# Causal attention in one fused kernel: one PSUM bank for output sums, four for max tiles, maxima turned inside the score ring, value product inside the slot

## What is computed

```python
# x: (8, 1024, 256); 16 heads of 16
qkv = einsum('bte,fe->btf', query, in_proj_weight).reshape(b, t, 3, H, D)
q = q / sqrt(D)
scores = einsum('bhqd,bhkd->bhqk', q, k)
scores = where(causal, scores, -inf)
attn = softmax(scores, axis=-1)
out = einsum('bhqk,bhkd->bhqd', attn, v)
out = einsum('bte,fe->btf', out.transpose(0, 2, 1, 3).reshape(b, t, e), out_proj_weight)
```

## Time and profile before

| | us |
|---|---|
| median of 3 runs | 1429.2 |
| lowest, highest | 1426.5, 1436.69 |
| the profiled execution | 1427.34 |
| its span, first to last instruction | 1425.6 |

### The profile page before, as it was taken

One profiled execution on the slowest core, in us unless ns is written; L12 is line 12 of the kernel. 1 busy time (PEld: TensorE's weight loads), 2 busy tenths in 40 slices (PEclk: granted clock), 3 DMA queues, 4 the chain that ended last, 5 costly groups with the idle time before them and its releaser, 6 DMA issues. The chain is left out here.

```text
span 1425.6 us, 38170 instructions
## 1 busy us (share of the span) xinstructions
PE 1301.0 (91%) x9260; PEld 831.4 (58%) x9260; DVE 1177.4 (83%) x4599; ACT 908.6 (64%) x1828; POOL 458.7 (32%) x877
## 2 busy tenths in 40 slices
PE   3999999979999999999999999999999995988885
PEld 3999889845444444444444444444444443877875
DVE  4788888758899999999999999999999982778786
ACT  3666666613777777777777777777777774444442
POOL 3333433211122222222222222122123123877772
PEclk9999999975999999999999999999999997998898
DMA  3466556943456456456356456456456444444441
GB/s 107 156 233 230 206 207 219 265 174 53 69 98 105 68 100 102 68 98 103 69 100 102 69 102 100 69 101 101 69 103 98 69 99 135 151 157 162 155 154 60
DMA packets 121898, 174.11 MB, mean 122 GB/s; under 512 B 44012, under 2 KB 71788, under 8 KB 121804
## 3 DMA queue, kind: packets, MB, share of 16 engines
q1 hardware_dynamic: 121816, 173.30, 52.1%
HBM read 96.08 MB, written 76.02 MB: 121 GB/s over the span
## 5 line engine op out<-in xcount | busy, mean ns | idle before, releaser
L973 ACT ACTIVATE b_probs<-bank 128x512 f32<-128x512 f32 x1152 | 595.3, 606 | 183.4 <-PE bank L1095 182.9
L1006 DVE CUSTOM_DVE_ANT_0 b_junk<-bank,mask 128x512 bf16<-128x512 f32 (+3 forms) x1032 | 447.9, 489 | 7.5 <-issue 7.5
L1009 DVE TENSOR_REDUCE b_pm<-bank 128x1 f32<-128x512 f32 x516 | 319.7, 683 | 28.4 <-PE bank L1077 28.4
L1077 PE MATMUL bank<-ks,qs 48*128 48x512 f32 (+3 forms) x1056 | 325.8, 409 | 7.2 <-PEq L435 6.3
L1095 PE MATMUL bank<-qs,ks 50*128 50x512 f32 (+3 forms) x1056 | 301.0, 389 | 20.2 <-ACT b_probs L973 13.4
L1111 PE MATMUL bank<-b_probs,b_vx 128*32 128x512 f32 (+3 forms) x3072 | 310.6, 500 | 3.1 <-POOL b_probs L941 2.0
L1095 PEld LDWEIGHTS bank<-qs,ks 50*128 50x128 f32 x1056 | 164.8, 189 | 214.2 <-ACT b_probs L973 196.8
L137 POOL TENSOR_TENSOR hold_pool<-zero 128x1 f32<-128x1 f32 x192 | 37.2, 194 | 675.4 <-ACT b_probs L973 675.3
L1077 PEld LDWEIGHTS bank<-ks,qs 48*128 48x128 f32 x1056 | 172.3, 195 | 54.6 <-DVE b_pm L1006 24.2
L941 POOL TENSOR_SCALAR_AFFINE_SELECT b_probs<-b_probs 128x512 f32<-128x512 f32 x256 | 158.3, 637 | 0.0
L1095 PE MATMUL bank<-b_qs,b_ks 50*128 50x512 f32 (+3 forms) x480 | 137.1, 382 | 9.7 <-ACT b_probs L973 6.5
(11 more groups left out here) (104 smaller groups left out, 2077.2 us busy)
## 6 DMA issues: line engine op xcount, KB each, us to landing
scr_qk<-a_qk SPq DMA_DIRECT2D x64, 512.0 KB, 3.2
qs<-scr_qk SPq DMA_DIRECT2D x132, 128.0 KB, 4.4
ks<-scr_qk SPq DMA_DIRECT2D x132, 128.0 KB, 4.9
scr_o<-b_o SPq DMA_DIRECT2D x64, 256.0 KB, 2.3
b_qs<-scr_qk SPq DMA_DIRECT2D x66, 128.0 KB, 4.0
b_ks<-scr_qk SPq DMA_DIRECT2D x66, 128.0 KB, 4.5
a_x<-x SPq DMA_DIRECT2D x16, 512.0 KB, 3.5
scr_x<-a_x SPq DMA_DIRECT2D x16, 512.0 KB, 2.7
```

The source lines that it names most:

```text
L973: act.activation(probs[:, s % NBUF, h, :], score_bank(t, last)[:], ACT.Exp).then_inc(p_ready, 1)
L1006: ins = dve.tensor_tensor_reduce(junk[:, t % SB, off:off + w], src, mask[:, BANK - w:BANK], 1.0, 0.0, ALU.add, ALU.max, pm[:, g.buf, 0, pl ...
L1009: ins = dve.tensor_reduce(pm[:, g.buf, 1, place(h), i:i + 1], src, AX.X, ALU.max)
L1077: last = pe.matmul(m_bank[t % SB][:, off:off + w], qs[g.buf][rows(h, SROWS), h // 2, i * P:(i + 1) * P], ks[g.buf][rows(h, SROWS), h // 2, ...
```

## The change

Five edits in stage B, and nothing outside it:

- **PSUM**: `o_bank` is one bank, which holds the low half until slot 2's product has been added and copied out, then the high half. Max tiles get four banks (`MB`).
- **Slots**: `SLOTS` is reordered so that all low-half work is in slots 0 to 2. Slots 1, 2 and 8 have two pieces. Slot 2 has pieces of both halves; its high piece is multiplied with slot 3, so slot 2's value product is 256 columns per head, slot 3's is 768, and its `probs` live in a fourth buffer.
- **Turn**: the turned maxima take a place in the score ring (between tiles 26 and 27) instead of a max bank. The turn is issued in slot 6 behind the value product.
- **Order in a slot**: score 0, max 0, score 1, max 1, max 2, score 2, value product (s-2), [turn], max 3, score 3. `S_ORDER` and `M_ORDER` are swapped.
- **ScalarE**: `out_o` and `out_m` move ahead of the slot's fourth exponential: the high half of g-1 in slot 1, the low half in slot 4 (before: behind slots 2 and 7), the turned maxima in slot 6 (before: behind slot 6).

GpSimd now masks slots 0, 1, 2, 7, 8 and spreads V behind slot 2.

```diff
-S_ORDER, M_ORDER = (0, 2, 1, 3), (1, 3, 0, 2)
+S_ORDER, M_ORDER = (1, 3, 0, 2), (0, 2, 1, 3)
 SLOTS = [
     [(0, 0, 512, 0)],
+    [(1, 128, 384, 0), (3, 384, 128, 384)],
+    [(2, 256, 256, 0), (6, 768, 256, 256)],
     [(0, 512, 512, 0)],
-    [(1, 128, 384, 0), (7, 896, 128, 384)],
-    [(2, 256, 256, 0), (6, 768, 256, 256)],
-    [(3, 384, 128, 0), (5, 640, 384, 128)],
     [(1, 512, 512, 0)],
     [(2, 512, 512, 0)],
     [(3, 512, 512, 0)],
     [(4, 512, 512, 0)],
+    [(5, 640, 384, 0), (7, 896, 128, 384)],
 ]
-LOW_DONE, HIGH_DONE = 4, 8
+LOW_DONE, HIGH_DONE = 2, 8
+VALUE_PIECES = [[(s, *piece) for piece in SLOTS[s] if (s > LOW_DONE) == (piece[1] >= BANK)] for s in range(NSLOT)]
+VALUE_PIECES[LOW_DONE + 1] += [(LOW_DONE, *piece) for piece in SLOTS[LOW_DONE] if piece[1] >= BANK]
+PROB_BUF = [s % 3 for s in range(NSLOT)]
+PROB_BUF[LOW_DONE] = 3
-SB = 3
-M_BANK = 2
-TURN_NEXT = SB * (GH // SB) + M_BANK
+SB, MB = 3, 4
+TURN_SLOT = NSLOT - AHEAD
+TURN_TILE = TURN_SLOT * GH + GH - 1
...
-        s_bank, m_bank, o_bank = psum[0:SB], psum[SB:2 * SB], psum[2 * SB:2 * SB + 2]
+        s_bank, m_bank, o_bank = psum[0:SB], psum[SB:SB + MB], psum[SB + MB]
...
+        def ring(g, t):
+            return g.k * (TILES + 1) + t + (t >= TURN_TILE)
+        def score_bank(g, t, last):
+            if last:
+                n = t % (SB + MB)
+                return m_bank[n - SB] if n >= SB else s_bank[ring(g, n) % SB]
+            return s_bank[ring(g, t) % SB]
+        def turn_bank(g):
+            return s_bank[(ring(g, TURN_TILE) - 1) % SB]
...
             def exp(g, s, last):
                 if not (g.first and s < NBUF):
                     act.wait_ge(pv_done, g.at(NSLOT, s - NBUF + 1))
                 for n, h in enumerate(S_ORDER):
+                    if n == GH - 1:
+                        if s == 1 and not g.first:
+                            out_o(g.next(-1), 1)
+                        if s == LOW_DONE + 2:
+                            out_o(g, 0)
+                        if s == TURN_SLOT and not last:
+                            out_m(g.next(1))
                     t = s * GH + n
                     act.wait_ge(s_tile, g.at(TILES, t + 1))
...
                     exp(g, s, last)
-                    if s == 2 and not g.first:
-                        out_o(g.next(-1), 1)
-                    if s == NSLOT - AHEAD and not last:
-                        out_m(g.next(1))
-                    if s == LOW_DONE + 3:
-                        out_o(g, 0)
...
             def turn_m(g):
                 pe.wait_ge(m_chain, g.at(3, 3))
-                pe.wait_ge(m_read, g.at(TILES, TILES + M_BANK + 1))
-                pe.transpose(m_bank[M_BANK][:, 0:P],
+                if g.k or not isinstance(g.r, int):
+                    p = g.next(-1)
+                    pe.wait_ge(p_ready, p.at(TILES, TURN_TILE - SB + 1))
+                    bank = turn_bank(p)
+                else:
+                    bank = s_bank[SB - 1]
+                pe.transpose(bank[:, 0:P],
...
             def max_tile(g, a, n):
-                if not (g.first and t < SB):
-                    pe.wait_ge(m_read, g.at(TILES, t - SB + 1))
-                if t == TURN_NEXT and not g.first:
-                    pe.wait_ge(m_out, g.at(1))
+                if not (g.first and t < MB):
+                    pe.wait_ge(m_read, g.at(TILES, t - MB + 1))
...
             def score_tile(g, s, n, last):
...
+                elif not last and TURN_TILE <= t < TURN_TILE + SB:
+                    if t == TURN_TILE + SB - 1:
+                        pe.wait_ge(m_out, g.at(1, 2))
+                    else:
+                        pe.wait_ge(p_ready, g.at(TILES, t - SB + 2))
                 elif not (g.first and t < SB):
                     pe.wait_ge(p_ready, g.at(TILES, t - SB + 1))
...
             def values(g, s):
-                if s < 2 and not g.first:
-                    pe.wait_ge(o_out, g.at(2, s - 1))
-                for j, q0, n, off in SLOTS[s]:
-                    half, col = q0 // BANK, q0 % BANK
+                    if not g.first:
+                        pe.wait_ge(o_out, g.at(2))
+                if s == LOW_DONE + 1:
+                    pe.wait_ge(o_out, g.at(2, 1))
+                pieces = VALUE_PIECES[s]
+                for n, (src, j, q0, w, off) in enumerate(pieces):
+                    col = q0 % BANK
                     for h in range(GH):
...
                 for s in range(NSLOT):
-                    for h in range(GH):
-                        score_tile(g, s, h, last)
-                        if s == NSLOT - AHEAD + 1 and h == 0 and not last:
-                            turn_m(g.next(1))
...
-                    if s >= 2:
-                        values(g, s - 2)
-                    elif not g.first:
-                        values(g.next(-1), NSLOT - 2 + s)
+                    score_tile(g, s, 0, last)
+                    maxima(s, 0)
+                    score_tile(g, s, 1, last)
+                    maxima(s, 1)
+                    maxima(s, 2)
+                    score_tile(g, s, 2, last)
+                    event(g, s)
+                    if s == TURN_SLOT and not last:
+                        turn_m(g.next(1))
+                    maxima(s, 3)
+                    score_tile(g, s, 3, last)
```

More of the change, by code:

```diff
@@ L958, in out_m @@
                     act.wait_ge(m_placed[p.buf], p.turn(32, 32))
-                act.copy(mt[:], m_bank[M_BANK][0:2 * GH * KT, 0:P]).then_inc(m_out, 1)
+                bank = turn_bank(g.next(-1)) if g.k or not isinstance(g.r, int) else s_bank[SB - 1]
+                act.copy(mt[:], bank[0:2 * GH * KT, 0:P]).then_inc(m_out, 1)
             def out_o(g, half):
@@ L964, in out_o @@
                     act.wait_ge(o_stored[half], g.at(16))
-                act.copy(o[:, half, :], o_bank[half][:]).then_inc(o_out, 1)
+                act.copy(o[:, half, :], o_bank[:]).then_inc(o_out, 1)
             def exp(g, s, last):
@@ L996, in maximum @@
                 t, h = a * GH + n, M_ORDER[n]
-                bank = m_bank[t % SB]
+                bank = m_bank[t % MB]
                 pieces = [(i, bank[:, off:off + w], w, off, k0 + w == (i + 1) * P) for i, k0, w, off in MAX_SLOTS[a]]
@@ L1071, in max_tile @@
                     pe.wait_ge(stacked[g.buf], g.turn(STACK, STACK))
-                if not (g.first and t < SB):
-                    pe.wait_ge(m_read, g.at(TILES, t - SB + 1))
-                if t == TURN_NEXT and not g.first:
-                    pe.wait_ge(m_out, g.at(1))
+                if not (g.first and t < MB):
+                    pe.wait_ge(m_read, g.at(TILES, t - MB + 1))
                 for i, k0, w, off in MAX_SLOTS[a]:
-                    last = pe.matmul(m_bank[t % SB][:, off:off + w], qs[g.buf][rows(h, SROWS), h // 2, i * P:(i + 1) * P],
+                    last = pe.matmul(m_bank[t % MB][:, off:off + w], qs[g.buf][rows(h, SROWS), h // 2, i * P:(i + 1) * P],
                                      ks[g.buf][rows(h, SROWS), h // 2, k0:k0 + w], start=True, stop=True)
@@ L1094, in score_tile @@
                 for j, q0, w, off in SLOTS[s]:
-                    done = pe.matmul(score_bank(t, last)[:, off:off + w], ks[g.buf][rows(h, SROWS_M), h // 2, j * P:(j + 1) * P],
+                    done = pe.matmul(score_bank(g, t, last)[:, off:off + w], ks[g.buf][rows(h, SROWS_M), h // 2, j * P:(j + 1) * P],
                                      qs[g.buf][rows(h, SROWS_M), h // 2, q0:q0 + w], start=True, stop=True)
@@ L1110, in values @@
                     for h in range(GH):
-                        last = pe.matmul(o_bank[half][2 * D * h:2 * D * (h + 1), col:col + n], vx[g.buf][:, j, h, :],
-                                         probs[:, s % NBUF, h, off:off + n], start=(j == 0),
-                                         stop=(s in (LOW_DONE, HIGH_DONE) and half == (s == HIGH_DONE)),
+                        last = pe.matmul(o_bank[2 * D * h:2 * D * (h + 1), col:col + w], vx[g.buf][:, j, h, :],
+                                         probs[:, PROB_BUF[src], h, off:off + w], start=(j == 0),
+                                         stop=(s in (LOW_DONE, HIGH_DONE) and n == len(pieces) - 1),
@@ L1114, in values, with event @@
                                          tile_position=(0, 2 * D * h))
                 last.then_inc(pv_done, 1)
[L1117 to L1132 removed]
+            def event(g, s):
+                if s >= 2:
+                    values(g, s - 2)
+                elif not g.first:
+                    values(g.next(-1), NSLOT - 2 + s)
@@ new lines, in step, with maxima @@
+            def step(g, last):
+                def maxima(s, n):
+                    if not last:
+                        a = s + AHEAD
+                        if a < NSLOT:
+                            max_tile(g.next(1), a, n)
+                        else:
+                            max_tile(g.next(2), a - NSLOT, n)
+                for s in range(NSLOT):
```

(2 more changed lines are left out.)

24 lines of the change are left out of this document (11 added, 13 removed).

## The result

| | us |
|---|---|
| before, median of 4 | 1429.15 |
| after, median of 4 (lowest, highest) | 1386.48 (1384.44, 1387.56) |
| ratio after / before, 95% interval | 0.969 (0.9652 to 0.9728) |
| profiled execution after, its span | 1387.56, 1385.8 |

The change saves 42.7 us. One of the four executions of the kernel of experiment 10 took 3447 us and is left out of its median. Windows of the kernel after, in the columns of the earlier trace rows: the steady stretch and one whole group.

A forecast was written before the change was run, and what follows sets the result against it. Bound: a closed loop through score bank, ScalarE and value product, 2.74 us a slot. 13.31 + 11.74 = 25.05 us a group against 26.68, times 31 groups, saves 50.5 us: 1379 us, forecast 1368 to 1390, range 1350 to 1408.

The forecast's parts named there:

- The plain slots: Slots 7, 8, 0, 1, 2: 2.61 us each, plus 0.11 for a copy, 0.15 for two-piece tiles; 13.31 together.
- Slots 3 to 6: VectorE becomes the pace; its reads and small steps, then the turn, take 11.74 us a group.
- 0.13 less, because max 2 now stands ahead of the waiting score 2: Last pair of a plain slot: product starts 0.43 us after score 2, loop 2.61 us instead of 2.74.
- the fourth max bank is what lets VectorE run on through the product: Slots 3 to 6: with four max banks VectorE keeps reading during the product, late by at most one tile.
- Moving the product mid-slot hides nothing by itself: Value product's place in the slot: the score loop is only rotated, so no time is gained.
- The turn: Slot 6, to be the longest: TensorE waits about 0.6 us for VectorE's last small step.
- Rival 4: Turn waits for VectorE, running a further lag behind (up to 2.1 us); 1444 us at the end; chance 0.06.
- Rival 1: Plain slots' loop stays at 2.74 us instead of 2.61; 1399 us; chance 0.18.
- Rival 2: More overlap than counted, no 0.15 or 0.11 us cost; 24.5 us a group, 1362 us; chance 0.13.
- Rival 3: q and k loads start later, behind the last score tile; a 1 us wait gives 1410 us; chance 0.08.
- Costed at nothing: Masks, `o_bank`, placing the maxima, first and last group, and clock were given no added time.
- nothing in the change makes TensorE idle longer: TensorE's clock: stays at 1.00 throughout, so no time was added for it.

The follow-up runs named there:

- experiment 10: Changed kernel with three max banks instead of four and score 2 ahead of max 2 again: 1442.0 us, ratio 1.011.
- experiment 1: Changed kernel with score 2 ahead of max 2 again, right before the value product: 1399.7 us, ratio 0.978.
- Experiments 2 and 3: 2: kernel before with max 3 issued ahead of score 3, 1451.0 us; 3: changed kernel with three max banks instead of four, 1447.2 us.
- experiment 6: Changed kernel with value product and turn at the slot's end again, three copies ahead of the next slot's first exponential: 1367.2 us, ratio 0.952.
- experiment 11: Changed kernel with VectorE's three small steps in a row ahead of its first read for the next group: 1364.0 us, ratio 0.956.
- ninth kernel: Kernel with product and turn at the slot's end, both output copies moved from ahead of the first exponential to ahead of the second: 1368.7 us, ratio 0.956.
- 4: Changed kernel with the turn behind max 0 of slot 7, the block copied behind slot 6's fourth exponential: 1371.9 us, ratio 0.957.
- 5: Changed kernel with both output copies behind the fourth exponential of slots 1 and 4: 1382.9 us, ratio 0.965.
- 7: Kernel with the turn behind max 0 of slot 7, its place in the score ring moved one tile on: 1363.6 us, ratio 0.951.
- 8: Kernel with the late turn and its ring place one tile on, plus both output copies behind the fourth exponential: 1361.4 us, ratio 0.950.
- 12: Kernel with VectorE's three small steps in a row, plus both output copies behind the fourth exponential: 1363.3 us, ratio 0.954.

## Why the prediction was right, and where it was off

The time, 1386.5 us, lies in the range, 7.5 us above the predicted 1379, and within the forecast's own 1368 to 1390. The gain was 42.7 us where 50.5 were worked out.

- **The plain slots.** 13.31 us worked out for five, 13.35 measured (510.33 to 523.68). Score 2 to product is 0.43 us as forecast; 2.61 a slot was 0.03 to 0.05 too low, and the 0.15 us set aside for two-piece tiles was too much by about as much.
- **Slots 3 to 6.** 11.74 worked out, 11.93 measured (25.28 less 13.35): this is the term that was mis-sized. VectorE was not busy throughout: it lost 0.11 us in slot 3, whose max 3 came late (read from 501.77, where its rhythm of 0.70 us a tile gives 501.66). From the third step's end to the turn it took 0.13 us, where I took 0.05 from another pair of engines. TensorE's wait was 0.80 us instead of "about 0.6". The odd products came out close to what was computed: 2.21 us for the slot with 256 columns (2.31 worked out), 3.35 for that with 768 (3.36).
- **Where the gain comes from** was half right. The step "0.13 less, because max 2 now stands ahead of the waiting score 2" named a true effect and gave it too much: 0.08 us by experiment 1, 13 us in all by the medians. The step "the fourth max bank is what lets VectorE run on through the product", priced in slots 3 to 6 only, is what failed as an explanation. Experiments 2 and 3 show a second loop through the max ring, of 2.77 to 2.97 us, which lengthens every slot but the turn's once max 2 is first. Only the fourth bank makes the new order pay: without it the change costs 19 us (about 9 of them by half-clock stretches), with it 43 are won. Even with the old order the fourth bank is worth 0.88 of the 1.40 us a group. I had checked each reader's release against four banks, and never closed the loop for three. The forecast of the time did not need that, the reason did.
- **"Moving the product mid-slot hides nothing by itself"** held, and more: with the turn in tow, and the copies, it costs 19 us (experiment 6).
- **The turn** was the longest slot and waited for VectorE, as said. Rival 4's extra lag did not come: the 0.80 us are the two reads ahead of the last step (experiment 11), not a backlog.
- **Rival 1** (2.74 a slot) fell, by the rows. **Rival 2**'s overlap did not come; the 0.11 us for the high half's copy did (slot 1 takes 2.77 us, 0.11 to 0.13 more than its neighbours). **Rival 3**: SyncE's first load of the next group starts at 516.56, 0.95 us after the last score tile (515.61; 0.91 worked out), and no wait for a load appears in the trace. Hidden, as worked out.
- **Costed at nothing**: the masks, V and the placed maxima show no wait on TensorE. The last group was not free. There the product of slot 3 waited 1.16 us for the low half's copy, the clock fell to 0.50 as it started, and ScalarE waited 1.72 us: from its first exponential to its last the group took 20.4 us (1123.5 to 1143.9) against 17.8 (1169.7 to 1187.5). The first groups gave 2.7 us more than 1.40 each. Most of that lies in the first period, 30.82 us before and 25.73 after, where the clock came back sooner: from 345 to 362 us it was granted at 0.52 before and at 0.86 after. That this cancels the last group's loss is luck; the prediction counted neither.
- **The clock** was granted at 1.00 through the steady stretch, as forecast. In the first and the last group it was not, and "nothing in the change makes TensorE idle longer" failed in the last.
- **One count was off** and changes no number: of the switches between half-array, transpose and product the turn's slot has four in the kernel before (two around the turn, two around the product) and three after, so one of four is saved, not one of three.

Experiment 1 puts 0.08 us a slot on a max tile queued behind a waiting score tile of the other row half, whose weights are loaded only 0.08 us behind the score tile's (512.57 against 512.49). The Trainium skill, "TensorE: Matmul & The Clock Gate", Part 3, The mechanism, says that a weight load for a free row group is pulled ahead of matmuls in flight. Read as covering a matmul that still waits, this would put the cost at nothing; the trace doesn't bear out that reading.

## What to carry to other kernels

Where an in-order engine fills a ring of n buffers and makes more than n entries between two long operations, the ring closes a loop through its reader and that operation; add up that loop for every ring before reading busy shares, because a queue's order pays only if the other rings leave room for it. A one-off step that must wait for another engine's chain (here the turn) belongs where the queue behind it would wait anyway, and the chain belongs ahead of that engine's other work. An edit that comes in a bundle with a good one, as the moved product did, is worth undoing by itself: here that gave 19 of the 25 us between the changed kernel and the best one measured. And an edit can cost time alone and save time beside another, as the new order does in the square of experiment 10, so try edits in pairs as well as one by one.

## What the runs showed of the hardware that was not expected

In the steady part of stage B TensorE's clock fell to half for some 3.4 us at a time in four of the kernels. Windows of the sixth kernel (columns as in the earlier trace rows):

```profile
498.00:499.00 1.00, 0.89 (x6) 0.47 (x6) 1.00 (x8) 1.00 (x3) 0.74 (x2) 1.00 0.01 4
499.00:500.00 1.00, 1.00 (x10) 0.26 (x12) 1.00 (x9) 0.79 (x2) 0.00 (x0) 0.54 0.00 0
500.00:501.00 1.00, 1.00 (x12) 0.34 (x8) 1.00 (x8) 0.00 (x0) 0.00 (x0) 0.50 0.00 0
501.00:502.00 1.00, 1.00 (x14) 0.20 (x4) 0.49 (x3) 0.00 (x0) 0.00 (x0) 0.50 0.00 0
502.00:503.00 1.00, 1.00 (x7) 0.72 (x7) 0.20 (x2) 0.36 (x1) 0.00 (x0) 0.76 0.00 0
```

The granted clock goes from 1.00 to 0.50 (2.4 to 1.2 GHz) and back. Before it fell TensorE was busy 0.89 of its last microsecond, with slot 5's score and max tiles; the product of 768 columns that follows (499.09) took 2.79 us instead of 1.50. Between 400 and 1080 us this came twice here, three times in the ninth kernel, four in the third and nine in the tenth, and never in the kernels before, after, or in 1, 2, 4, 5, 7, 8, 11 and 12. Each time costs about 1.5 us. All 18 lie on slot 3's product of 768 columns, which starts between 0.1 us before the fall and 0.9 us behind it; the other groups have the same product and keep the clock. Why these kernels and not their neighbours stays open: the changed kernel waits 0.8 us at each turn and keeps its clock. In the last group of the changed kernel a wait of 1.16 us stands ahead of 3.4 us at 0.50, again on that product.
